# A two-layer network on one core: last output products begun early, expert weights loaded early, scatters spaced, sixteen wide products ahead of the attention

## The chip, the core and the metric

The kernel runs on one core of one Trainium2 chip. The metric is the device time of one execution in microseconds; three runs of the kernel before gave 2939.88, 2945.26 and 2947.61 us, median 2945.26 us. TensorE (PE) multiplies matrices, VectorE (DVE) and ScalarE (ACT) work element by element, GpSimd (POOL) does some products and the indirect transfers, SyncE (SP) issues the other transfers. Each engine runs its own list of instructions in order; they meet at semaphores.

## What is computed

Two layers on an input of 4 batches x 1024 tokens x 256 values. Everything is in float32.

```python
h = layernorm(x) * (1 + ca) + sa
x = x + ga * mamba(h)            # layer 0: state-space scan, 512 inner channels, 16 states
h = layernorm(x) * (1 + cb) + sb
x = x + gb * moe0(h)             # 8 experts, hidden 384, top 2
h = layernorm(x) * (1 + ca) + sa
x = x + ga * attention(h)        # layer 1: 8 heads of 128, causal, T = 1024
h = layernorm(x) * (1 + cb) + sb
x = x + gb * moe1(h)             # 16 experts, hidden 512, top 2, 640 slots each
```

The last step of the state-space layer is `y @ W_out`. In the second expert layer each token's normalised row goes, with its weights and its number, to two slots of a table in device memory; expert e reads its 640 slots, and adds its results to the tokens' rows of the output.

## The kernel before

Five phases follow one another, with a meeting of all engines between them: the state-space layer (`phase_mamba`, up to 973 us), routing of layer 0 (`phase_route`), its experts (`phase_experts0`, up to 1377 us), the attention with the routing of layer 1 inside it (`phase_attention`, 1377 to 2624 us), and the experts of layer 1 (`phase_experts1`, to the end). In each phase the order of every engine's work is written out by hand.

**State-space layer.** The 4096 tokens are 8 chunks of 512 columns (`CHUNKS`), two for each batch. A chunk has 64 scan steps (`STEPS`); step s takes the accumulator bank `da_ps[s % 4]`. VectorE scans and multiplies by C into `hc`, TensorE sums the results into `y_ps` (`sum_states`), ScalarE copies them out (`take_y`), TensorE turns them (`turn_back`), ScalarE copies again (`take_back`), GpSimd multiplies by the gate (`gate_y`, L796, one call for each half of the 512 inner channels), and `out_product` (L472) multiplies by W_out: for each of 4 token tiles, 4 products of 256 columns and one with the identity that adds x, in the banks `proj_ps`. `take_out` (L664) copies a pair of tiles back to x. For a chunk that isn't the last all this lies beside the next chunk's scan; for the last one it stands at the end of the phase, and `store_x` and the meeting of the engines follow.

**Attention, start.** SP issues four loads of 512 KB, for each half of batch 0 one from `sums0` (to `sh.x`) and one from `more0`, which are to be added; their semaphores are `x_first[0]` and `x_first[1]`. Behind them come the modulation rows (1.5 MB), `gate_w` (16 KB), `pos` (512 KB), `w_o` (1 MB, L1745) and batch 1's rows (1 MB). VectorE's `stats(0, j)` adds tile j and takes its statistics, for 8 tiles; then variance, root, reciprocal; then `normalise_rows` makes the 8 tiles' rows (a ring of 4). TensorE's list in this phase begins with these waits, ahead of everything else it does:

```python
pe.wait_ge(sh.att_w_in, 16)     # L1827
pe.wait_ge(S["w_o_in"], 16)     # L1828
```

Then it waits for `gate_w`, turns the 8 tiles' rows (`turn_rows`, L1837, two products of 128 columns a tile in one bank, which ScalarE copies to `h_b` before the next), and starts `project` (L1906) with eight products of 512 columns for the first head's q and k. The profile shows each float32 product as two instructions (these eight are "x16"), and each turn (transpose) as one.

**Attention, a batch.** Four batches, batches 1 and 2 being two turns of one loop. A batch has N = 64 steps n (8 heads x 8 row tiles): TensorE `score(n)`, VectorE `maximum(n)` (L2276), ScalarE the exponential, VectorE the division, TensorE `turn(n)`, ScalarE the copy (L2064), TensorE `weigh` (L1946). Between them stand the next batch's rows (`turn_rows`, from n = 56) and the routing of the batch before. The latter ends in `slots` at n = 54; then GpSimd's `scatter(b - 1)` (L1798) issues 16 indirect transfers of 128 rows each (L1803) in one go and waits until they have landed. After the last step `output` multiplies by `w_o`. Batch 3's own rows are routed in a tail, with 16 more scatters, and then the phase ends.

**Second expert phase, start.** SP issues the gate rows (512 KB, into `sh.mods[:, 2]`), then for experts 0 and 1 the slots (`xs`, 650 KB) and the two weights (512 KB each). TensorE turns the 5 slot tiles of expert 0 (L1546) and then multiplies (`hidden`, L1557).

## Time and profile before

The profiled execution took 2948.64 us, its span (first to last instruction) is 2946.9 us; this is 3.4 us above the median of the three runs.

| what | value |
|---|---|
| runs of the kernel before | 2939.88 / 2945.26 / 2947.61 us |
| profiled execution | 2948.64 us, span 2946.9 us |
| mean granted TensorE clock | 0.931 of full |
| busy: PE, DVE, ACT, POOL | 85%, 71%, 44%, 42% |
| phases end at | 973, 1377, 2624, 2947 us |

Busy time is summed over the span. Idle time of an engine matters only where another one waits for it, so the argument goes by stretches in order of time. A granted clock of 1.00 is 2.4 GHz, one of 0.50 is 1.2 GHz. In the rows, "[5.35 <-issue]" is the engine's idle time before the instruction and what ended it; "remote" is a semaphore event for which the profile has no instruction at that time.

### The profile page before, as it was taken

To read this page: it belongs to the slowest core of one execution; us is meant where nothing else is said; L and a number is where in the kernel's file an instruction comes from. 1 tells how busy PE (TensorE), PEld (TensorE's weight loads), DVE (VectorE), ACT (ScalarE), POOL (GpSimd) and SP (SyncE) were. 2 spreads that over 40 slices of the span, in tenths; PEclk is the share of its full clock that TensorE was granted. 3 is DMA by queue.
4 is the path that set the end of the run, shared out by engine and by line. 5 is a ranking of instruction groups with operands and counts; after the bars stand their busy time and mean duration, and the time that the engine had idled before them with its cause. 6 is when DMAs were issued, how large, how long until landed. Compare 5 with 4: busy or idle time off the path is not lost.

```text
span 2946.9 us, 39189 instructions
## 1 busy us (share of the span) xinstructions
PE 2494.0 (85%) x12341; PEld 1785.8 (61%) x12342; DVE 2104.0 (71%) x4277; ACT 1296.8 (44%) x2563; POOL 1234.6 (42%) x531
## 2 busy tenths in 40 slices
PE   6667777877866679996999999989998999859998
PEld 4355555555555469995566666556665666547776
DVE  4999999999999566665667477737774667455554
ACT  4667777677765245553343234313432343211111
POOL 2799999999997046664000000100001000223444
PEclk8889989888977889998999999999999999869999
DMA  4645655654655434345000100000000000035554
GB/s 146 202 151 177 194 169 171 196 167 168 201 171 165 161 104 63 63 63 140 18 1 1 45 3 1 18 28 19 1 6 28 15 1 1 29 108 128 129 129 73
DMA packets 150845, 268.98 MB, mean 91 GB/s; under 512 B 18316, under 2 KB 107324, under 8 KB 150172
## 3 DMA queue, kind: packets, MB, share of 16 engines
q1 hardware_dynamic: 121916, 227.12, 24.2%
q0 software_dynamic: 28224, 37.78, 7.7%
q8 instruction: 81, 1.33, 0.2%
q10 hardware_dynamic: 544, 2.10, 0.2%
q14 instruction: 80, 0.66, 0.1%
HBM read 209.52 MB, written 57.43 MB: 91 GB/s over the span
## 4 chain that ended last, share of the span: by engine, by line
PE 44%; DVE 3%; issue 2%; another core or an unknown queue 1%; ACT 1%; DMA 1%; POOL 0%; DVEq 0%; SPq 0%; ACTq 0%; POOLq 0%
PE at_o_ps L1946 8%; PE at_s_ps L1922 8%; PE at_qk_ps L1906 6%; PE e_h_ps L1557 5%; PE e_y_ps L1568 5%; PE at_s_ps L1954 4%; PE at_pt_ps L1933 4%; PE at_qk_ps L1911 3%; PE at_s_ps L1906 1%; DVE at_small L2276 1%; PE e_x_ps L1546 0%; PE at_s_ps L1911 0%; PE at_qk_ps L1837 0%; PE at_qk_ps L1852 0%
## 5 line engine op out<-in xcount | busy, mean ns | idle before, releaser
L765 POOL TENSOR_TENSOR dbx<-u,b_all 128x2048 f32<-128x2048 f32 x128 | 578.6, 4535 | 69.6 <-DVE u L844 34.1
L1803 POOL DMA_INDIRECT slots<-at_r_rows,slot_of x64 | 63.0, 984 | 1179.3 <-DVE slot_of L2218 1084.1
L2064 ACT COPY at_pt<-at_pt_ps 128x512 f32<-128x512 f32 (+3 forms) x384 | 172.2, 483 | 543.0 <-PE at_pt_ps L1933 507.6
L649 ACT ACTIVATE da_ps<-delta,a_neg 128x512 f32<-128x512 f32 x512 | 347.9, 689 | 134.9 <-DVE hc L917 126.7
L469 PE MATMUL y_ps<-ident,hc 128*128 128x128 f32 x1536 | 241.6, 301 | 90.7 <-DVE hc L917 90.2
L1922 PE MATMUL at_s_ps<-at_qk 128*128 128x512 f32 (+3 forms) x768 | 293.9, 492 | 3.3 <-DVE at_v L2267 3.1
L1946 PE MATMUL at_o_ps<-at_pt,at_v 128*128 128x512 f32 (+3 forms) x768 | 294.0, 495 | 0.0
L469 PEld LDWEIGHTS y_ps<-ident,hc 128*128 128x128 f32 x1536 | 196.0, 155 | 144.9 <-DVE hc L917 117.5
L2053 ACT ACTIVATE at_probs<-at_s_ps,at_small 128x128 f32<-128x128 f32 (+7 forms) x256 | 192.1, 751 | 202.0 <-DVE at_small L2278 201.6
L917 DVE TENSOR_TENSOR hc<-da_ps,c_all 128x512 f32<-128x512 f32 x384 | 257.0, 671 | 0.0
L907 DVE TENSOR_TENSOR_SCAN da_ps<-da_ps,state,dbx 128x512 f32<-128x512 f32 x192 | 243.0, 1275 | 6.1 <-ACT da_ps L649 4.3
L907 DVE TENSOR_TENSOR_SCAN da_ps<-da_ps,dbx 128x512 f32<-128x512 f32 x192 | 231.8, 1216 | 11.4 <-ACT da_ps L649 7.8
L2274 DVE TENSOR_TENSOR at_s_ps<-at_s_ps,at_later 128x128 f32<-128x128 f32 x256 | 75.9, 297 | 210.2 <-PE at_s_ps L1922 193.7
L1922 PEld LDWEIGHTS at_s_ps<-at_qk 128*128 128x128 f32 x768 | 138.1, 192 | 129.2 <-issue 97.1
L1906 PE MATMUL at_qk_ps<-at_h_b,w_qkv 128*128 128x512 f32 x448 | 211.9, 595 | 1.5 <-DVE at_rank L2204 0.9
L1534 POOL DMA_INDIRECT out<-e_ys,e_row_i x80 | 125.3, 1566 | 193.6 <-DVE e_ys L1643 164.4
L2276 DVE TENSOR_REDUCE at_small<-at_s_ps 128x1 f32<-128x128 f32 (+7 forms) x256 | 194.0, 758 | 8.8
L1933 PE MATMUL at_pt_ps<-ident,at_probs 128*128 128x128 f32 x1152 | 171.2, 276 | 32.8 <-ACT at_pt L2064 11.7
L1933 PEld LDWEIGHTS at_pt_ps<-ident,at_probs 128*128 128x128 f32 x1152 | 137.6, 142 | 98.9 <-issue 78.5
L1946 PEld LDWEIGHTS at_o_ps<-at_pt,at_v 128*128 128x128 f32 x768 | 129.3, 194 | 61.2 <-issue 58.3
L1591 ACT ACTIVATE e_hid<-e_h_ps 128x320 f32<-128x320 f32 x128 | 56.0, 437 | 249.5 <-PE e_h_ps L1557 249.0
L1568 PE MATMUL e_y_ps<-e_w,e_hid 128*128 128x256 f32 x640 | 152.3, 382 | 5.6 <-ACT e_hid L1591 5.6
(385 smaller groups left out, 5003.8 us busy)
## 6 DMA issues: line engine op xcount, KB each, us to landing
b_all<-bc_rows SPq DMA_DIRECT2D x128, 512.0 KB, 4.5
c_all<-bc_rows SPq DMA_DIRECT2D x128, 512.0 KB, 5.1
e_w<-L_ffn_w SPq DMA_DIRECT2D x32, 512.0 KB, 5.5
slots<-zeros SPq DMA_DIRECT2D x40, 260.0 KB, 6.3
e_xs<-slots SPq DMA_DIRECT2D x16, 650.0 KB, 7.1
w<-L_ffn_W SPq DMA_DIRECT2D x24, 384.0 KB, 8.4
more<-zeros SPq DMA_DIRECT2D x16, 256.0 KB, 5.0
sums<-x SPq DMA_DIRECT2D x8, 512.0 KB, 6.9
```

The lines of the kernel that those rows point to most:

```text
L469: mm = nc.tensor.matmul(y_ps[par][:, at], source[:, at], sh.ident[:], start=False, stop=(last and j == CT - 1), is_transpose=True)
L649: nc.scalar.activation(da_ps[s % RING_DA][:], delta[:, c % 2, m, :], ACT.Exp, scale=sh.a_neg[:, m, n:n + 1]).then_inc(S["da_ready"], 1)
L765: nc.gpsimd.tensor_tensor(dbx[:, at % RING_DBX], pair, rows, ALU.mult).then_inc(S["dbx_ready"], 1)
L907: nc.vector.tensor_tensor_scan(out, h, dbx[:, at % RING_DBX, i // 2, par, :], 0.0 if c % CPB == 0 else state[:, s:s + 1], ALU.mult, ALU.ad ...
L917: nc.vector.tensor_tensor(hc[:, v % RING_H, :], da_ps[s % RING_DA][:], c_all[:, at % RING_C, s % GS // 2, :], ALU.mult).then_inc(S["hc_rea ...
L1568: last = nc.tensor.matmul(y_ps[(r + t) % 2][:], hid[:, m, t * P:(t + 1) * P], w2[:, r, m, :], start=(m == 0), stop=(m == MF1 - 1))
L1906: last = nc.tensor.matmul(out, w_qkv[:, k, h, i // 2, :], h_b[:, i % 2, k, :], start=(k == 0), stop=(k == KE - 1))
L1922: last = nc.tensor.matmul(s_ps[n % 2][:, part * CH:end], qk[:, h % 2, 0, i * P:(i + 1) * P], qk[:, h % 2, 1, part * CH:end], start=True, s ...
L1933: last = nc.tensor.transpose(pt_ps[half][:, j % CT, :], probs[:, n % 3, j * P:(j + 1) * P], sh.ident[:])
L1946: last = nc.tensor.matmul(o_ps[:, first:], v[:, h % 2, j, :], pt[half][:, j, first:], start=(j == 0), stop=(j == (half + 1) * CT - 1))
L2053: nc.scalar.activation(probs[:, n % 3, 0:(i + 1) * P], s_ps[n % 2][:, 0:(i + 1) * P], ACT.Exp, bias=small[:, n % 4, 1:2], scale=SCALE, acc ...
L2276: nc.vector.reduce_max(small[:, n % 4, 0:1], s_ps[n % 2][:, 0:(i + 1) * P], AX_X).then_inc(S["max_taken"], 1)
```

## The change

1. State-space layer, last chunk: of each token tile's five products the three that don't need the second half of the gated values (x by the identity, two of the four W_out products) are issued earlier, into `da_ps[0]` and `da_ps[1]`: tiles 0 and 1 after the summing of steps 61 and 62, tiles 2 and 3 after `turn_back`. After the last gating only two products for each tile are left. `take_out` of that chunk reads `da_ps`.
2. Attention, start: SP waits for `x_first[1]` before it issues the modulation rows and what follows. VectorE adds the first half in one operation of 1024 columns, GpSimd the second half. TensorE gets 16 products of 512 columns (`WARM`) on `w_qkv`, whose results nobody reads, between its first waits (L1827, L1828) and its wait for `gate_w`.
3. Attention, batches 1 to 3: before scattering tile j of the batch before, GpSimd waits until `score` of step 54 + j is done (`SLOTS[2]` is 54).
4. The weights of experts 0 and 1 and the gate rows of the second expert phase go to the room of `w_qkv`, and are loaded in batch 3, when the last `project` is done; SP waits for them before the phase ends. In the second expert phase SP then issues only the slots for experts 0 and 1.

The diff, without lines that only rename:

```diff
@@ phase_mamba, tensor
+            def last_first_blocks(j):
+                pair, i = j // 2, j % 2
+                if i == 0:
+                    pe.wait_ge(S["hc_ready"], hc_at(LAST, STEPS - RING_DA + pair) + 1)
+                    pe.wait_ge(S["y_gated"], LAST * HALVES + 1)
+                    pe.wait_ge(S["w_ready"], B)
+                out = da_ps[pair][:, i * E:(i + 1) * E]
+                nc.tensor.matmul(out, sh.ident[:], sh.x[:, LAST * CT + j, :], start=(i == 0), stop=False, skip_group_check=True)
+                for k in range(2):
+                    nc.tensor.matmul(out, u[:, LAST % 2, k, j * P:(j + 1) * P], sh.w_out[:, k, :], start=False, stop=False, skip_group_check=True)
+
+            def last_blocks(pair):
+                if pair == 0:
+                    pe.wait_ge(S["y_gated"], CHUNKS * HALVES)
+                for i in range(2):
+                    j = pair * 2 + i
+                    for k in range(2, MD):
+                        mm = nc.tensor.matmul(da_ps[pair][:, i * E:(i + 1) * E], u[:, LAST % 2, k, j * P:(j + 1) * P], sh.w_out[:, k, :],
+                                              start=False, stop=(k == MD - 1), skip_group_check=True)
+                mm.then_inc(S["out_done"], 1)
...
                     sum_states(c, k)
+                    if c == LAST and k >= STEPS - 3 and k < STEPS - 1:
+                        last_first_blocks(k - STEPS + 3)
...
-                turn_back(CHUNKS - 1, m)
+                turn_back(LAST, m)
+            for j in range(2, CT):
+                last_first_blocks(j)
             for pair in range(2):
-                out_product(CHUNKS - 1, pair)
+                last_blocks(pair)
@@ phase_experts1, sync
-            sp.dma_start(sh.mods[:, 2], d["mod_rows"][1, 5].partition_broadcast(P)).then_inc(mods_in, 16)
...
-                if not early(e, 2):
-                    sp.wait_ge(y_done, (e - 1) * S1)
+                if early(e, 2):
+                    return
+                sp.wait_ge(y_done, (e - 1) * S1)
@@ phase_attention, sync
+            sp.wait_ge(x_first[1], 32)
             load_mods(sp, d, sh, 1, 0, S["mods_in"])
...
             store_out(B - 2)
+            sp.wait_ge(S["qk_done"], B * HEADS * PIECES + 1)
+            sp.dma_start(sh.gates[:], d["mod_rows"][1, 5].partition_broadcast(P)).then_inc(sh.gates_in, 16)
+            for e in range(2):
+                sp.dma_start(sh.w1[:, e], d["L1_ffn_w1"][e].rearrange("(k p) f -> p k f", p=P)).then_inc(sh.w1_in[e], 16)
+                sp.dma_start(sh.w2[:, e], d["L1_ffn_w2"][e].rearrange("(m p) f -> p m f", p=P)).then_inc(sh.w2_in[e], 16)
             store_out(B - 1)
@@ phase_attention, gpsimd
+            late = slice(CT, TPB)
+            pool.wait_ge(x_first[1], 32)
+            nc.gpsimd.tensor_tensor(sh.x[:, late], sh.x[:, late], more[:, late], ALU.add).then_inc(first_summed[1], 1)
...
                 for j in tiles:
                     i = rb * TPB + j
+                    if count is None:
+                        pool.wait_ge(S["scored"], (rb + 1) * N + SLOTS[2] + 1 + j)
@@ phase_attention, tensor
             pe.sem_inc(S["rows_left"], 1)
+            for i in range(WARM):
+                nc.tensor.matmul(s_ps[0][:, 0:CH], w_qkv[:, 0, 0, 0, :], w_qkv[:, 0, 0:2, 0:2, :], start=True, stop=True)
             pe.wait_ge(S["gate_in"], 16)
@@ phase_attention, vector
+            early = slice(0, CT)
+            dve.wait_ge(x_first[0], 32)
+            nc.vector.tensor_tensor(sh.x[:, early], sh.x[:, early], more[:, early], ALU.add).then_inc(first_summed[0], 1)
             for j in range(TPB):
-                stats(0, j)
+                if j % CT == 0:
+                    dve.wait_ge(first_summed[j // CT], 1)
+                nc.vector.bn_stats(sh.stats[:, j, :], sh.x[:, j, :]).then_inc(S["stats_in"], 1)
+            dve.sem_inc(S["summed"], TPB)
```

## Rows read from the trace of the kernel before

**Rows 1.** The page's chain that ended last, shares of the span.

```profile
PE 44%; DVE 3%; issue 2%; another core or an unknown queue 1%; ACT 1%; DMA 1%; POOL 0%; DVEq 0%; SPq 0%; ACTq 0%; POOLq 0%
```

**Rows 2.** Order of time, first phase's end: start us, us, engine, line.

```profile
958.61 2.34 POOL L796 TENSOR_TENSOR u<-u,gate 128x1024 f32<-128x1024 f32 x1 [13.08 <-ACT u L581]
...
961.00 3.49 PE L479 MATMUL proj_ps<-w_out,u 128*128 128x256 f32 x8 [3.09 <-POOL u L796]
...
971.44 0.58 ACT L667 COPY x<-proj_ps 128x512 f32<-128x512 f32 x1 [3.73 <-PE proj_ps L481]
```

**Rows 3.** Stretch, length, busy us (instructions) by engine, granted clock, DMA.

```profile
961.00:964.20 3.20, 3.20 (x8) 2.62 (x9) 0.00 (x0) 0.00 (x0) 0.00 (x0) 0.52 0.00 0
964.20:971.30 7.10, 7.10 (x34) 6.00 (x32) 0.75 (x2) 0.58 (x1) 0.00 (x0) 1.00 0.00 0
```

**Rows 4.** TensorE in order of time, short bursts.

```profile
919.04 0.66 PE L469 MATMUL y_ps<-ident,hc 128*128 128x128 f32 x4 [1.12 <-DVE hc L917]
921.47 1.12 PE L469 MATMUL y_ps<-ident,hc 128*128 128x128 f32 x4 [1.77 <-DVE hc L917]
```

**Rows 5.** Transfers at the attention's start: KB, us to landing.

```profile
x<-sums SPq DMA_DIRECT2D x1, 512.0 KB, 3.9
...
at_attn<-more SPq DMA_DIRECT2D x1, 512.0 KB, 7.4
...
at_w_o<-woT SPq DMA_DIRECT2D x1, 1024.0 KB, 12.9
```

**Rows 6.** The attention's start in order of time.

```profile
1379.01 0.51 SPq L1741 DMA_DIRECT2D at_attn<-more  x1
...
1381.67 0.44 SPq L1745 DMA_DIRECT2D at_w_o<-woT  x1
...
1392.38 0.48 DVE L2243 SCALAR_TENSOR_TENSOR at_rows<-at_rows,rstd,mods 128x256 f32<-128x256 f32 x1
...
1394.96 0.66 PE L1837 MATMUL at_qk_ps<-ident,at_rows 128*128 128x128 f32 x2 [24.46 <-DVE at_rows L2243]
...
1404.57 8.72 PE L1906 MATMUL at_s_ps<-at_h_b,w_qkv 128*128 128x512 f32 x16 [0.46 <-ACT at_h_b L2039]
```

**Rows 7.** Batch 1, in order of time, while batch 0 is scattered.

```profile
1901.80 1.05 POOL L1803 DMA_INDIRECT slots<-at_r_rows,slot_of  x1 [521.99 <-DVE slot_of L2218]
...
1911.30 0.38 PE L1837 MATMUL at_qk_ps<-ident,at_rows 128*128 128x128 f32 x2
...
1912.78 1.09 PE L1933 MATMUL at_pt_ps<-ident,at_probs 128*128 128x128 f32 x8 [0.24 <-issue]
...
1919.71 0.58 ACT L2064 COPY at_pt<-at_pt_ps 128x512 f32<-128x512 f32 x1 [6.05 <-remote]
...
1921.44 0.96 POOL L1803 DMA_INDIRECT slots<-at_r_rows,slot_of  x1 [0.30 <-issue]
...
1924.73 0.69 DVE L2290 COPY at_attn<-at_o_ps 128x512 f32<-128x512 f32 x1 [6.59 <-remote]
```

**Rows 8.** Row maximum of steps 54 and 63, batches 0, 1, 3.

```profile
1612.29 1.09 DVE L2276 TENSOR_REDUCE at_small<-at_s_ps 128x1 f32<-128x896 f32 x1
...
1641.36 1.23 DVE L2276 TENSOR_REDUCE at_small<-at_s_ps 128x1 f32<-128x1024 f32 x1
...
1902.82 1.09 DVE L2276 TENSOR_REDUCE at_small<-at_s_ps 128x1 f32<-128x896 f32 x1
...
1944.14 1.23 DVE L2276 TENSOR_REDUCE at_small<-at_s_ps 128x1 f32<-128x1024 f32 x1
...
2505.30 1.09 DVE L2276 TENSOR_REDUCE at_small<-at_s_ps 128x1 f32<-128x896 f32 x1
...
2546.58 1.23 DVE L2276 TENSOR_REDUCE at_small<-at_s_ps 128x1 f32<-128x1024 f32 x1
```

**Rows 9.** The second expert phase's start in order of time.

```profile
2624.31 0.43 SPq L1507 DMA_DIRECT2D e_xs<-slots  x1
...
2630.45 1.12 PE L1546 MATMUL e_x_ps<-ident,e_xs 128*128 128x128 f32 x4 [23.57 <-DMA e_xs<-slots]
```

More of the change, by code:

```diff
@@ L482, in out_product @@
                 mm.then_inc(S["out_done"], 1)
+            LAST = CHUNKS - 1
+            def last_first_blocks(j):
[17 more added lines that the diff above has]
+                mm.then_inc(S["out_done"], 1)
             pe.wait_ge(S["c_ready"], 1)
@@ L666, in take_out @@
                 act.wait_ge(S["out_done"], c * 2 + pair + 1)
-                nc.scalar.copy(sh.x[:, tile:tile + 2, :], proj_ps[pair][:].rearrange("p (i e) -> p i e", i=2)).then_inc(S["out_added"], 1)
+                bank = da_ps[pair] if c == CHUNKS - 1 else proj_ps[pair]
+                nc.scalar.copy(sh.x[:, tile:tile + 2, :], bank[:].rearrange("p (i e) -> p i e", i=2)).then_inc(S["out_added"], 1)
             act.dma_start(wmod[0], d["L0_wmod"].rearrange("(k p) f -> p k f", p=P)).then_inc(wmod_in[0], 16)
@@ L1464, in phase_experts1 @@
         sem = sh.kept("e1_")
-        w1 = sb("w1", [P, 2, KE, F1])
-        w2 = sb("w2", [P, 2, MF1, E])
+        w1, w2, gates = sh.w1, sh.w2, sh.gates
         xs = sb("xs", [P, 2, S1, ROW])
@@ L1478, in phase_experts1 @@
         y_ps = [ps(f"y_ps{i}", [P, E]) for i in range(2)]
-        w1_in, w2_in, x_in = ([sem(f"{n}{i}") for i in range(2)] for n in ("w1_in", "w2_in", "x_in"))
-        mods_in, consts_ready, steps_set, meta_chain, gate_chain, rows_set, added = (
-            sem(n) for n in "mods_in consts_ready steps_set meta_chain gate_chain rows_set added".split())
+        w1_in, w2_in, x_in = sh.w1_in, sh.w2_in, [sem(f"x_in{i}") for i in range(2)]
+        consts_ready, steps_set, meta_chain, gate_chain, rows_set, added = (
+            sem(n) for n in "consts_ready steps_set meta_chain gate_chain rows_set added".split())
         x_turned, x_copied, h_done, h_act, y_done, y_copied = (sem(n) for n in "x_turned x_copied h_done h_act y_done y_copied".split())
@@ L1622, in gate_rows @@
             def gate_rows(e, r, b):
-                before = sh.mods[:, 2, 0, :]
+                before = gates[:, 0, :]
                 for t in range(S1):
@@ L1646, in body @@
                     read_meta(e + 1, 1 - r, q + r)
-            dve.wait_ge(mods_in, 16)
+            dve.wait_ge(sh.gates_in, 16)
             for b in range(1, B):
-                nc.vector.tensor_tensor(sh.mods[:, 1, b, :], sh.mods[:, 2, b, :], sh.mods[:, 2, b - 1, :], ALU.subtract).then_inc(steps_set, 1)
+                nc.vector.tensor_tensor(sh.mods[:, 1, b, :], gates[:, b, :], gates[:, b - 1, :], ALU.subtract).then_inc(steps_set, 1)
             dve.wait_ge(consts_ready, 2)
@@ L1708, in phase_attention @@
         x_first = [sem(f"x_first{th}") for th in range(CPB)]
+        first_summed = [sem(f"first_summed{th}") for th in range(CPB)]
         names = ("x_in summed route_in gate_in stats2_in stats2_chain var2_ready std2_ready rstd2_ready r_half_ready r_row_ready r_turned_done "
@@ L1716, in phase_attention @@
         block = ctx.enter_context(nc.Block(no_gpsimd_drain=True))
+        WARM = 16
         ADD = tuple(4 + 2 * j for j in range(TPB))
@@ L1769, in _ @@
             store_out(B - 2)
+            sp.wait_ge(S["qk_done"], B * HEADS * PIECES + 1)
[3 more added lines that the diff above has]
+                sp.dma_start(sh.w2[:, e], d["L1_ffn_w2"][e].rearrange("(m p) f -> p m f", p=P)).then_inc(sh.w2_in[e], 16)
             store_out(B - 1)
             sp.wait_ge(S["x_stored"], 16 * B)
+            sp.wait_ge(sh.gates_in, 16)
+            for e in range(2):
+                sp.wait_ge(sh.w1_in[e], 16)
+                sp.wait_ge(sh.w2_in[e], 16)
         @block.gpsimd
@@ L2114, in stats @@
                 tile = nb * TPB + j
-                if isinstance(nb, int) and nb == 0:
-                    dve.wait_ge(x_first[j // CT], 32)
-                else:
-                    dve.wait_ge(S["x_in"], nb * 32)
+                dve.wait_ge(S["x_in"], nb * 32)
                 nc.vector.tensor_tensor(sh.x[:, tile, :], sh.x[:, tile, :], more[:, j, :], ALU.add).then_inc(S["summed"], 1)
@@ L2478, in program @@
             phase_experts0(nc, d, sh)
+        place = sh.w_qkv[:].rearrange("p k h c f -> p (k h c f)")
+        sh.w1 = place[:, 0:2 * KE * F1].rearrange("p (r k f) -> p r k f", r=2, k=KE)
+        sh.w2 = place[:, 2 * KE * F1:2 * KE * F1 + 2 * MF1 * E].rearrange("p (r m e) -> p r m e", r=2, m=MF1)
+        sh.gates = place[:, 2 * KE * F1 + 2 * MF1 * E:2 * KE * F1 + 2 * MF1 * E + B * E].rearrange("p (b e) -> p b e", b=B)
+        sh.w1_in, sh.w2_in = ([sh.kept("e1_")(f"{n}{i}") for i in range(2)] for n in ("w1_in", "w2_in"))
+        sh.gates_in = sh.kept("e1_")("gates_in")
         phase_attention(nc, d, sh)
```

## The prediction

> **What bounds the kernel now.** I read the chain that ended last first: no engine but TensorE holds a large share of it [rows 1]. So an edit pays where TensorE waits, and by no more than that wait. Then I read four places in order of time, those that the change touches: the end of the first phase [rows 2, 3], the start of the attention [rows 5, 6], the end of each batch, where the rows of the batch before are scattered [rows 7, 8], and the start of the last phase [rows 9]. The reader is to see in each what released TensorE, and at which of its two clocks it then worked: [rows 3] has 8 instructions of 256 columns in 3.20 us at a granted clock of 0.52 (0.4 each), and 34 in 7.10 us at 1.00 (0.21 each). A float32 product is two such instructions.
>
> **Part 1, last output products.** Before, TensorE starts them at 961.00, released by the gating on GpSimd, and ScalarE starts the last copy at 971.44: 10.4 us for 40 instructions [rows 2]. After it, 8 products (16 instructions) are left: 3.4 us at full clock plus 0.2 to the copy. The other 12 products of W_out and x move ahead. Those of tiles 0 and 1 stand between the sums of steps 61, 62 and 63: 6 instructions of 0.215 = 1.3 us twice, of which TensorE's waits there take up some; the last sum, the copy, the turn and the gating come later by about 1.7 us. Those of tiles 2 and 3 (2.6 us) lie beside the gating of 2.34 us [rows 2] and keep TensorE at work, so that the clock, which fell there before, stays. Sum: 1.7 + 3.4 + 0.2 - 10.4 = -5 us. Bounds: -1.7 if the clock falls all the same (16 x 0.4 = 6.9), -6 if the early products delay the gating by less. The next phase starts earlier by as much, nothing else waits.
>
> **Part 2, the attention's start.** Who released TensorE's first turns at 1394.96? The profile names VectorE's row, but that row started at 1392.38 and took 0.48, so it had been ready for 2 us [rows 6]. The transfer of `w_o`, issued at 1381.67, took 12.9 us: it landed at 1394.6 [rows 5, 6]. TensorE's list begins with the wait for it (L1828). That wait stays, and the 16 products stand behind it, not in the time in which TensorE is idle. So they are on the path.
> When does `w_o` land now? The loads of batch 0 end at 1379.01 + 7.4 = 1386.4; before, what followed was queued already, now it is issued only then. The first load of 512 KB took 3.9 us from issue [rows 5]; it was issued 1.5 us ahead of the fourth, so it landed at 1381.4, and the other three followed at 1.7 us each. So about 2.2 us of the 3.9 are start-up. `w_o` lands at 1396.9, TensorE starts at 1397.2. The new adding doesn't reach so far: GpSimd's operation of 128x1024 takes 2.34 us [rows 2], so it is done at 1388.8; before, adding, statistics, variance and the first row together took from the landing at 1386.4 to 1392.9 [rows 5, 6], and 6.5 us from 1388.8 is 1395.3, still ahead of `w_o`.
> The 16 products are 32 instructions of 512 columns. By [rows 3], doubled, one takes 0.85 us at half clock and 0.43 at full. A model of the start stands in [rows 6]: the first 16 of `project` take 8.72 us from an idle engine, which is 4 of 0.85 and 12 of 0.43 and the end of the last one. So 3.4 + 28 x 0.43 = 15.4 us, to 1412.7. What do they give back? A turn of two instructions takes 0.66 us cold [rows 6] and 0.38 warm [rows 7]; with ScalarE's copy a tile takes 1.21 and would take 0.93, so 8 tiles save 2.2 us if the clock holds, and the first 16 instructions of `project` would take 6.9 instead of 8.6. But the clock doesn't hold in such sparse work: in [rows 4] four turns of 128 columns stand alone with idle time of 1.1 and 1.8 us ahead of them, at 919.04 at full clock (0.66) and at 921.47 at half (1.12). I take half of the first gain and none of the second: 8 x 1.07 = 8.6, then 8.6: 1429.9, where before it was 1404.57 + 8.56 = 1413.1. That is +16.8; with all gained back it is +13.9, with `w_o` no later +11.6, with nothing gained back +17.8. I take +16. Behind it TensorE is the bound, so it is not given back.
>
> **Part 3, the scatters.** From [rows 8]: from the row maximum of step 54 to that of step 63 batch 0 takes 29.1 us, batch 1 41.3, batch 3 41.3 (batch 2 repeats it). Batch 0 alone has no scatters. The excess is 12.2 us three times, 37 us. [Rows 7] show it: 16 transfers are issued back to back, 1.3 us apart, from 1901.80 to 1922.4. Nothing is late in the first 9 us. Then TensorE's turns of 1912.78 end at 1913.9, and ScalarE, idle for 6 us, copies them at 1919.71; VectorE is idle for 6.6 us until 1924.73, which is 2.3 us after the last issue has ended. In the view of waits, those that end "remote" occur nowhere in the kernel but in these three stretches. I read it as TensorE's signals being delayed by an unbroken run of scatters.
> By the change the first four go at once (5 us), then GpSimd waits for step 56 (about 4 us), then each pair of 2.5 us is let go by a step; batch 0's steps are 29.1 / 9 = 3.2 us apart, those of the short row tiles (56 to 59) less, I estimate 2.5. So there is another nearly unbroken run of about 8, and if signals are late then, `score` is late too, GpSimd stops within one pair and the delay clears in the 2.3 us seen above. I put what is left at one such episode, 3 us a batch. Sum: 3 x (3 - 12.2) = -28 us. Bounds: -37 with nothing left; 0 if spacing doesn't matter. The rows are scattered later (the last pair at step 61), but the next user of `r_rows` comes 30 steps on. A gain below this one isn't possible: nothing else of it is on TensorE's path.
>
> **Part 4, early weights.** SP waits for the last `project` of batch 3 with only the store of that batch behind it, which is due after `output`; 2.5 MB lie under the attention, and at worst make batch 3's scatters slower. In the last phase the slots are issued first, 0.4 us sooner, and alone: before, the issue at 2624.31 released TensorE at 2630.45, after 6.1 us [rows 9]; the first load of 512 KB in [rows 5] took 3.9, so 650 KB take some 4.3. -2 us, between -0.4 and -2.3; the weights were never late.
>
> **Sum.** -5 + 16 - 28 - 2 = -19 us on 2948.6 gives 2929.6 for such an execution; the profiled one lies 3.4 us above the median, so 2926 us.
>
> **The rivals**, all on the median.
> The stall goes wholly: part 3 gives -37, total -28, 2917 us. For it: the first eight transfers in a row delayed nothing [rows 7]. Against: some eight come in a row again.
> The stall is tied to a place in the order of instructions (code that has to be fetched, say), and scatters only lengthen it: then the run at steps 56 to 58 meets it as before and only the end of the run is cut, about -15, total -6, 2939 us. For it: it begins at about the same steps in all three batches.
> Spacing changes nothing and the 16 products cost what they cost: part 3 gives 0, total +9, 2954 us, slower than before. It decides from the point where part 3 gives less than 9 us, which is what the other parts cost together. For it: between two pairs GpSimd hardly pauses from step 56 to 59. Against: the pauses before it, and that `score` holds the scatters back.
> A worse form: every one of the six later pairs delays one signal by 2.4 us or more, so that the steps and the scatters hold each other up; 17 us a batch instead of 12.2, total +23, 2968 us.
> The Trainium skill (SBUF — State Buffer, section Who interferes with whom) says that a DMA never contends with a compute engine, and that PE and ACT wait on nobody. By it the scatters couldn't stall TensorE or ScalarE, spacing them would give 0 and the kernel would come to the 2954 us of the third rival; the rows speak against the rule as far as signals are concerned, since the same steps take 12 us more only beside scatters.
>
> **How the numbers follow.** Chances: forecast 0.42, stall gone 0.28, tied to a place 0.12, nothing from spacing 0.11, worse form 0.07. A measurement of this kernel tells 0.3% (8.8 us) from no change. Faster by more: the first two, and a little of the third, 0.73. Within: the rest of the third and half of the fourth, 0.14. Slower: 0.13. The range is to hold the first three: its low end is -37 with +12, -6 and -2, so 2911; its high end is the third with +18 at the start, 2942. With a margin for both, 2909 to 2943 us.
>
> **What the profile would show.** Part 1: TensorE starts on `da_ps` at about 962.7 and the last copy at 966.3, clock 1.00. Part 2: 32 instructions of 512 columns starting at 1397, not before 1394; `project` ends its 16 at about 1430 less what part 1 gave (5). If they start at 1378, the wait was not what I took it for, and part 2 is near -1. Part 3: the steps 54 to 63 of batches 1 to 3 in 32 us, "remote" waits gone or one of 2 to 4 us each, scatters in pairs. 41 us there would make the forecast wrong by itself. Part 4: the last phase's first turn 4 to 5 us after its first issue.

## The result, and the profile after

The changed kernel took 2920.78 us (median of 4 runs, 2920.41 to 2922.07), the kernel before 2944.66 us in the same comparison (4 runs, 2939.88 to 2947.61): ratio 0.992, 95% interval 0.9907 to 0.9934. That is 23.9 us less; forecast were 19 less, 2926.0 us. The profiled executions span 2920.4 and 2946.9 us, so 26.5 us have to be found in the two traces.

A later experiment showed that this result doesn't hold on every chip: on another the same changed kernel is 10.9 us slower than the kernel before. Both are told below, the first comparison first.

Where the 26.5 us went, from the first transfer of each stage to that of the next:

| stage | before | after | difference |
|---|---|---|---|
| first phase, up to its last copy (ScalarE) | 971.44 | 970.82 | -0.6 |
| from there to the attention's first transfer | 406.1 | 404.2 | -1.9 |
| from there to the product group behind the first `project` | 35.6 | 55.1 | +19.4 |
| from there to the last phase's first transfer | 1210.8 | 1169.6 | -41.2 |
| from there to the first hidden product | 10.2 | 8.0 | -2.2 |

**First phase's end.** The changed kernel in order of time (start us, us, engine, line); these rows answer to [rows 2].

```profile
957.79 1.27 DVE L935 TENSOR_TENSOR_SCAN da_ps<-da_ps,state,dbx 128x512 f32<-128x512 f32 x1
...
964.65 2.35 POOL L824 TENSOR_TENSOR u<-u,gate 128x1024 f32<-128x1024 f32 x1 [14.68 <-ACT u L608]
...
967.06 3.72 PE L503 MATMUL da_ps<-w_out,u 128*128 128x256 f32 x16 [0.51 <-POOL u L824]
...
970.82 0.59 ACT L695 COPY x<-da_ps 128x512 f32<-128x512 f32 x1 [1.14 <-PE da_ps L503]
```

16 instructions are left behind the gating instead of 40, and they run in 3.72 us, so at full clock. From the scan of step 63 to the last copy it is 13.0 us; before, the same scan stood at 953.36, 18.1 us ahead of the copy at 971.44. That is the gain of 5 us. But the scan itself stands 4.4 us later than before, in code that the change doesn't touch (2.8 us of it are there at 253 us, all of it at 595 us); so only 0.6 us is left in this pair of executions. Such a difference says nothing of the change: over the 14 profiled executions of this document that scan starts anywhere between 953.3 and 957.8 us. From it to the last copy it is 18.1 to 19.4 us in the nine that have the old end of this phase, and 13.0 to 13.3 in the five that have the new one.

**The attention's start**, in order of time; these rows answer to [rows 6].

```profile
1374.98 0.37 SPq L1768 DMA_DIRECT2D x<-sums  x1
...
1385.55 0.48 SPq L1774 DMA_DIRECT2D at_w_o<-woT  x1
...
1391.29 0.48 DVE L2286 SCALAR_TENSOR_TENSOR at_rows<-at_rows,rstd,mods 128x256 f32<-128x256 f32 x1
```

TensorE alone:

```profile
1395.98 16.86 PE L1936 MATMUL at_s_ps<-w_qkv 128*128 128x512 f32 x32 [27.71 <-DMA at_w_o<-woT]
1412.67 0.38 PE L1881 MATMUL at_qk_ps<-ident,at_rows 128*128 128x128 f32 x2
1413.61 0.41 PE L1881 MATMUL at_qk_ps<-ident,at_rows 128*128 128x128 f32 x2 [0.55 <-ACT at_h_b L2085]
...
1419.38 0.66 PE L1881 MATMUL at_qk_ps<-ident,at_rows 128*128 128x128 f32 x2 [0.55 <-ACT at_h_b L2085]
1420.51 9.69 PE L1952 MATMUL at_s_ps<-at_h_b,w_qkv 128*128 128x512 f32 x16 [0.46 <-ACT at_h_b L2085]
```

The wide products stand behind the transfer of `w_o`, as the profile now says itself, and the first normed row, finished at 1391.8, waits for them until 1412.67. What the clock did (stretch, length, busy us (instructions) of each engine, granted clock, DMA):

```profile
1395.90:1401.90 6.00, 5.92 (x7) 2.53 (x8) 0.00 (x0) 0.00 (x0) 0.00 (x0) 0.51 0.88 281
1401.90:1412.60 10.70, 10.70 (x26) 4.70 (x25) 0.00 (x0) 0.00 (x0) 0.00 (x0) 1.00 0.00 0
1412.60:1419.40 6.80, 2.93 (x16) 1.39 (x14) 3.75 (x8) 2.61 (x7) 0.00 (x0) 0.96 0.10 32
...
1421.00:1425.00 4.00, 4.00 (x6) 1.42 (x6) 0.57 (x1) 0.76 (x1) 0.00 (x0) 0.50 0.52 183
```

The products do raise the clock to its upper level (1.00 of 2.4 GHz) and the turns have it nearly to their end. But the turns keep TensorE busy for 2.93 us of 6.80 only, the clock falls at their end, and `project` starts at the lower level: its 16 instructions take 9.69 us, against 8.72 in [rows 6].

**The scatters.** The row maxima of steps 54 and 63 of batches 1 and 3 on VectorE, in order of time; these rows answer to [rows 8].

```profile
1919.74 1.09 DVE L2325 TENSOR_REDUCE at_small<-at_s_ps 128x1 f32<-128x896 f32 x1
...
1948.03 1.23 DVE L2325 TENSOR_REDUCE at_small<-at_s_ps 128x1 f32<-128x1024 f32 x1
...
2495.74 1.09 DVE L2325 TENSOR_REDUCE at_small<-at_s_ps 128x1 f32<-128x896 f32 x1
...
2522.02 1.23 DVE L2325 TENSOR_REDUCE at_small<-at_s_ps 128x1 f32<-128x1024 f32 x1
```

28.3, 28.3 and 26.3 us in batches 1 to 3 instead of 41.3, 41.8 and 41.3: 41.2 us in all. No wait that ends "remote" is left in these stretches; a few signals of TensorE are still late there, the two worst by 1.1 and 1.3 us, in batch 3. Batch 3 is shorter than batch 0 (29.1), which has no scatters; so batch 0 was not the right measure of what an undisturbed batch takes.

**The last phase**, in order of time; these rows answer to [rows 9].

```profile
2599.66 7.89 SPq L1532 DMA_DIRECT2D e_xs<-slots  x3
...
2603.99 1.11 PE L1572 MATMUL e_x_ps<-ident,e_xs 128*128 128x128 f32 x4 [21.73 <-DMA e_xs<-slots]
```

4.3 us from issue to the first turn, against 6.1 before. The forecast had 4.3.

### The profile page after: what moved, and what is told of

Same layout as the page of the kernel before. It is cut to its first block and busy times, and to the rows that moved or that the text cites. A ratio compares the mean times of both kernels' runs of the same rounds, so it can differ in the third digit from the quotient of the medians.

```text
span 2920.4 us, 39254 instructions
## 1 busy us (share of the span) xinstructions
PE 2500.7 (86%) x12373; PEld 1788.7 (61%) x12374; DVE 2101.7 (72%) x4270; ACT 1297.2 (44%) x2563; POOL 1238.3 (42%) x532
## 5 line engine op out<-in xcount | busy, mean ns | idle before, releaser
L469 PE MATMUL y_ps<-ident,hc 128*128 128x128 f32 x1536 | 239.4, 300 | 83.6 <-DVE hc L945 82.8
L1979 PEld LDWEIGHTS at_pt_ps<-ident,at_probs 128*128 128x128 f32 x1152 | 136.1, 141 | 75.4 <-issue 52.2
L1979 PE MATMUL at_pt_ps<-ident,at_probs 128*128 128x128 f32 x1152 | 168.8, 274 | 11.7 <-DVE at_probs L2335 11.4
L802 POOL TENSOR_TENSOR own_h<-own_h,c_all 128x2048 f32<-128x2048 f32 x32 | 144.9, 4527 | 31.3 <-DVE own_h L935 31.3
```

The lines of the kernel that those rows point to most:

```text
L469: mm = nc.tensor.matmul(y_ps[par][:, at], source[:, at], sh.ident[:], start=False, stop=(last and j == CT - 1), is_transpose=True)
L1979: last = nc.tensor.transpose(pt_ps[half][:, j % CT, :], probs[:, n % 3, j * P:(j + 1) * P], sh.ident[:])
```

## The experiments

The kernels ran in four groups, each group on one chip of its own, with the kernel before timed beside it. The chip of the first comparison is called A, those of the groups B, C, D and E (whether A is one of the others isn't known). By "the hold" I mean what [rows 7] show: signals between engines that arrive some microseconds late beside a run of scatters, as waits that end "remote".

The traces also tell whose signals are late. Each semaphore event can be set beside the end of the last instruction that raises that semaphore. In the kernel before on A, from the first scatter of a batch to 4 us behind the last, 39 events of TensorE are recorded and 28 of them come over 0.3 us late, the worst 11.3 us; of the 78 of VectorE and ScalarE none does. In the eight traces from C, D and E none of TensorE's 635 is late. So it is TensorE's signals that are held, and no other engine's. (TensorE's ends are modelled by the profile, so how much of each delay lies ahead of the signal can't be told from them alone; run 2 speaks to that.)

### Chip B: which part brings what

**1. The spaced scatters alone**, added to the kernel before:

```
             for j in tiles:
                 i = rb * TPB + j
+                if count is None:
+                    pool.wait_ge(S["scored"], (rb + 1) * N + SLOTS[2] + 1 + j)
                 for k in range(2):
                     nc.gpsimd.indirect_dma_start(...)
```

> The kernel before with the spaced scatters alone: one added wait per token tile, nothing else of the change. My theory, that a long unbroken run of scatters delays the signals of the other engines: the row maxima of steps 54 and 63 lie about 28.3 us apart in all four batches (before 29.1, 41.3, 41.8, 41.3), the time falls by 41 us to about 2904 us. Rival, that the delay hangs on a place in the order of instructions and that other parts of the change (the shifted code, the products ahead of the attention) removed it: steps 54 to 63 still take 35 us or more in three batches, the time stays over 2925 us.

Measured 2908.11 us, the kernel before 2948.87 beside it: ratio 0.9865 (0.9849 to 0.9882), -40.8 us. Steps 54 to 63 take 29.4, 28.4 and 26.4 us. So this one wait brings what the whole change brought in these steps, and no other part of the change has a share in it. A remnant of the hold is still to be seen in batch 1, of 1.6 us, behind no more than four scatters in a row:

```profile
1917.15 0.27 ACT L2066 COPY at_pt<-at_pt_ps 128x128 f32<-128x128 f32 x1 [1.59 <-remote]
1917.29 0.96 POOL L1805 DMA_INDIRECT slots<-at_r_rows,slot_of  x1 [1.08 <-remote]
```

**2. One unbroken run, begun later.**

```
+                if count is None and j == 0:
+                    pool.wait_ge(S["scored"], (rb + 1) * N + 63)
```

> The kernel before, with all 16 scatters of a batch still in one unbroken run, but begun only once score 62 of the next batch is made (one wait ahead of the first scatter). My theory, unbroken run: steps 54 to 63 take 28.3 us, and the delay comes back behind step 63, in the output products and the first products of the batch behind; the time stays within 12 us of the kernel before. Rival, place in the order of instructions (steps 54 to 63 are what is delayed, by whatever runs beside them): nothing is delayed later, the time falls by some 41 us to about 2904 us. Second rival, sheer number of scatters beside the steps: also no gain from spacing alone, which the first run answers.

Measured 2911.4 us, ratio 0.9881 (0.9865 to 0.9898): -37.5 us, where my theory wanted the delay back behind step 63. By its time alone the rival had won. The trace (end of the run of scatters in batch 1, order of time) says otherwise:

```profile
1928.66 1.01 POOL L1805 DMA_INDIRECT slots<-at_r_rows,slot_of  x1 [549.14 <-PE at_s_ps L1924]
...
1938.13 7.17 PE L1956 MATMUL at_s_ps<-at_w_o,at_attn 128*128 128x256 f32 x32 [1.60 <-issue]
...
1945.15 5.75 PE L1948 MATMUL at_o_ps<-at_pt,at_v 128*128 128x512 f32 x16
...
1948.25 0.96 POOL L1805 DMA_INDIRECT slots<-at_r_rows,slot_of  x1 [0.30 <-issue]
1951.65 0.42 DVE L2418 TENSOR_TENSOR at_gated<-at_s_ps,mods 128x256 f32<-128x256 f32 x1 [6.83 <-remote]
```

VectorE waits for the second group of output products, which TensorE ended at 1945.3 before it went straight on to other work; so here TensorE isn't held, its signal is. VectorE is held for 6.8 us until 2.4 us behind the end of the last issue, as at 1924.73 in [rows 7], where it was 2.3. The same is seen in batch 2 (6.8 us) and in batch 3 (4.4 us), and nothing is held in steps 54 to 63 (28.7, 28.7 and 25.4 us). So the hold went with the scatters, away from the steps: it isn't tied to a place in the order of instructions. It cost only 0.8 us there (from the maximum of step 63 to the first of the next batch 53.0 instead of 52.2), since TensorE worked on through it: the output products go into four banks in turn, and VectorE catches up. In steps 54 to 63 TensorE, VectorE and ScalarE hand every tile to each other, and TensorE itself comes to stand, as in batch 1 of the kernel before (TensorE alone):

```profile
1914.27 0.81 PE L1922 MATMUL at_s_ps<-at_qk 128*128 128x384 f32 x2
1920.44 0.45 PE L1933 MATMUL at_pt_ps<-ident,at_probs 128*128 128x128 f32 x1 [5.35 <-issue]
```

The expectation was right in the mechanism and wrong in the price.

**3. Without the wide products** (`WARM = 0` in the changed kernel).

> The changed kernel without the sixteen wide products. My theory: they run whole behind the wait for w_o and on the path, so the turned rows begin as soon as w_o lands (21 us behind the attention's first transfer), are turned at half clock in 1.21 us each as before, and the projections that follow take 8.7 us: the next product group begins about 16 us earlier, time about 2905 us. Rival: the products were hidden, since rows, mods or w_o would have held the turned rows as long, or a higher clock behind them repays them: time within 4 us of the changed kernel, 2917 to 2925 us.

Measured 2904.66 us, ratio 0.9856 (0.9839 to 0.9872). The changed kernel wasn't in this group, so the price is read in the trace, from the attention's first transfer:

| us from the first transfer to | first turn | `project` | next product group |
|---|---|---|---|
| kernel before (A) | 17.5 | 27.1 | 35.6 |
| changed kernel (A) | 37.7 | 45.5 | 55.1 |
| changed kernel (D) | 36.0 | 44.2 | 52.9 |
| without wide products (B) | 20.9 | 30.5 | 39.3 |
| and wait for `w_o` late (B) | 16.5 | 26.1 | 35.5 |
| wide products, wait for `w_o` late (C) | 17.9 | 26.0 | 35.2 |

Without the products the start is 15.8 us shorter than in the changed kernel on A and 13.6 shorter than on D: they were wholly on the path. TensorE's row without them:

```profile
1391.45 0.66 PE L1881 MATMUL at_qk_ps<-ident,at_rows 128*128 128x128 f32 x2 [27.78 <-DMA at_w_o<-woT]
...
1401.06 8.98 PE L1952 MATMUL at_s_ps<-at_h_b,w_qkv 128*128 128x512 f32 x16 [0.46 <-ACT at_h_b L2085]
```

**4. Without them, and the wait for `w_o` where `w_o` is read.**

```
-            pe.wait_ge(S["w_o_in"], 16)
...
                     if t == 0:
+                        if first_batch:
+                            pe.wait_ge(S["w_o_in"], 16)
                         pe.wait_ge(S["exp_done"], b * N + N - 1)
```

> The changed kernel without the sixteen wide products, and with TensorE's wait for w_o moved from the attention's start to its first output product, where w_o is first read. My theory: the start is then held by the first normed row, ready 16.8 us behind the attention's first transfer instead of 21.0 for w_o: about 4 us below the changed kernel without wide products, 20 us below the changed kernel, about 2901 us. Rival: another transfer (the gate's weights, the modulation rows) holds TensorE as long as w_o did: time as without the wide products, about 2905 us.

Measured 2901.03 us, ratio 0.984 (0.9823 to 0.9856), 3.6 us below run 3. TensorE's first turn is now really released by the row, which the profile had named in the kernel before too:

```profile
1389.90 0.66 PE L1880 MATMUL at_qk_ps<-ident,at_rows 128*128 128x128 f32 x2 [23.24 <-DVE at_rows L2287]
```

So the wait for `w_o` had cost 4.4 us of the start (20.9 against 16.5). In the kernel before it was 2.1: the first row ready at 15.4, the turn at 17.5 [rows 6]; the changed order of loads had doubled it.

### Chip C: wide products that do lie beside the loads, and a surprise

**5. Run 4 with its wide products.**

> The changed kernel with its sixteen wide products kept, and TensorE's wait for w_o moved from ahead of them to the first output product, so that they start at once and really lie beside the loads. My theory: 16.9 us of products from the phase's start end about when the first normed row is ready (16.5 us behind the first transfer); the turns behind them run at full clock, 0.96 us each instead of 1.21, for some 7 us, which gives at most 2 us back, and the clock falls before the projections as in the changed kernel: the same time as without wide products, 2901 us within 2 us. Rival: the full clock holds into the projections, and the start is 4 us or more shorter: below 2898 us. Second rival: they end later than the first row and cost 3 us or more: above 2904 us.

Measured 2898.73 us (7 runs, 2896.44 to 2902.62). TensorE in order of time:

```profile
1374.51 16.50 PE L1935 MATMUL at_s_ps<-w_qkv 128*128 128x512 f32 x32 [8.50 <-issue]
1390.85 0.38 PE L1880 MATMUL at_qk_ps<-ident,at_rows 128*128 128x128 f32 x2
...
1398.88 9.41 PE L1951 MATMUL at_s_ps<-at_h_b,w_qkv 128*128 128x512 f32 x16 [0.46 <-ACT at_h_b L2086]
```

The turns take 8.0 us instead of 9.6, but start 1.4 us later, and `project` is as slow as without (9.3 us to the next product group, 9.4 in run 4): 0.3 us gained in all (35.2 against 35.5). The first theory holds in the trace; the time lies 0.3 us below the stretch that it gave (2901 us within 2), and most of the distance to run 4 is the chip, for the rest of the attention takes 3.2 us less here than in run 4, which had a remnant of the hold. Even where they lie beside the loads, the wide products bring next to nothing, because the clock falls in the sparse turns before the dense work begins.

The surprise was the kernel before: 2907.2 us on this chip (10 runs, 2904.85 to 2909.28), 37 to 42 us less than on A and B. Run 5 gains 8.5 us on it, ratio 0.9973 (0.9961 to 0.9984).

**6 to 8. Three patterns to find what the hold depends on:** twelve scatters and four, a filler behind each scatter (`nc.gpsimd.memset(filler[:], 0.0)`), and 64 rows in each scatter (`sh.slot_of[0:64, k, i:i + 1]`, `r_rows[0:64, j, :]`; half of the rows aren't stored).

> The kernel before, with twelve scatters of a batch unbroken (15 us) and the last four held until score 60 of the next batch. My theory (signals of other engines are held from about 10 us into an unbroken run to about 2.4 us behind its last scatter): the hold begins as before but ends some 5 us earlier, so steps 54 to 63 take 33 to 35 us in batches 1 to 3, between the 28.3 of the spaced kernel and the 41.3 of the kernel before; about 2925 us. Rival, a place in the order of instructions or an effect of the total number: 28 to 29.5 us or 40 us or more.

> The kernel before, with no wait for scores, but one short fill of a scratch tile of 128x256 behind each scatter on the same engine (0.3 us), so that the scatters start every 1.6 us instead of 1.27 and never stand directly behind each other. Theory A, the average rate counts (about what the spaced kernels have, 16 in 26 us): no signal is held, steps 54 to 63 take 28 to 29.5 us, about 2908 us. Theory B, only real pauses of the engine count (a wait of 0.65 us or more each pair): signals are still held, steps 54 to 63 take 38 us or more, over 2935 us.

> The kernel before, with each scatter of batches 0 to 2 writing 64 rows instead of 128, so that half of those rows are never stored; still 16 scatters back to back. If the number of rows (descriptors, written one by one) fills something up: a scatter takes less time and the hold vanishes, steps 54 to 63 take 28 to 30 us, about 2908 us. If each scatter instruction counts whatever its rows: its duration stays near 0.96 us with a pitch of 1.27 us, and steps 54 to 63 stay at 41 us, about 2948 us.

Measured 2909.62, 2909.19 and 2907.71 us, one run each. Steps 54 to 63: 28.6, 28.8 and 25.4 us; 29.1, 29.2 and 25.6; 28.9, 28.8 and 25.4. As the kernel before ran without the hold too, none of the three tells anything of its cause. The last has all sixteen scatters unbroken, 1.2 us apart, with nothing late; so not the pattern made the difference to A and B, but the chip (or something else that changed from group to group with it).

### Chip D: the changed kernel where the hold is missing

**9. The changed kernel once more, and 10. twelve and four once more.**

> The changed kernel itself, once more. In the call before this one the kernel before took 2907 us on its chip instead of 2945 to 2949, so the hold of signals during the scatters seems to be missing on some chips. Theory: what the change does to the attention's start, the last output products and the last phase (worked out from the traces: +19.4, -6.9 and -2.2 us) is there on every chip, and only the 41 us of the scatters depends on the chip. If this chip has the hold (kernel before 2940 us or more), the changed kernel takes 2919 to 2923 us, 24 to 28 us less than the kernel before; if it has not (kernel before near 2907 us), the changed kernel takes 2917 to 2921 us and is 10 to 14 us slower than the kernel before. Rival: the difference between the chips lies elsewhere and both kernels move alike: the changed kernel near 2883 us where the kernel before takes 2907.

> Twelve scatters unbroken, the last four held until score 60, once more, since the chip of its first run showed no held signals at all. If this chip has the hold: steps 54 to 63 take 33 to 35 us in batches 1 to 3 if signals are held from about 10 us into an unbroken run to about 2.4 us behind its last scatter (about 2925 us); 28 to 29.5 us if the hold is tied to a place or to the number of sixteen. If this chip has no hold: 28.7 us and 25.4 us in the last batch, as in the first run, about 2909 us.

The kernel before took 2908.23 us (10 runs), so this chip lacks the hold as well. The changed kernel took 2919.1 us (7 runs, 2914.89 to 2920.71): ratio 1.0035, interval 1.0024 to 1.0047. It is slower, by 10.9 us, as the first theory had it. Its rows, TensorE at the attention's start and VectorE's maxima of steps 54 and 63 of batch 1:

```profile
1391.08 15.61 PE L1936 MATMUL at_s_ps<-w_qkv 128*128 128x512 f32 x32 [27.44 <-DMA at_w_o<-woT]
1406.53 0.38 PE L1881 MATMUL at_qk_ps<-ident,at_rows 128*128 128x128 f32 x2
...
1414.75 8.87 PE L1952 MATMUL at_s_ps<-at_h_b,w_qkv 128*128 128x512 f32 x16 [0.46 <-ACT at_h_b L2085]
```

```profile
1913.15 1.09 DVE L2325 TENSOR_REDUCE at_small<-at_s_ps 128x1 f32<-128x896 f32 x1
...
1941.80 1.23 DVE L2325 TENSOR_REDUCE at_small<-at_s_ps 128x1 f32<-128x1024 f32 x1
```

The steps take 28.7 us, in batch 3 25.4, with spacing as without it. Twelve and four took 2905.34 us (one run), steps 28.6, 28.6 and 25.4: again nothing on the cause. But its trace is that of the kernel before on this same chip in all but the scatters, so the two can be set side by side: their spans are 2903.6 and 2913.2 us, the changed kernel 9.6 longer. Up to the attention's first transfer it gains 6.4, its start costs 17.0 more (52.9 against 35.9), the rest of the attention gains 0.2, the last phase's start 1.7, and what follows takes 0.9 more. The profiled execution is the fastest of the seven, 4.2 us below their median, so this doesn't settle the 10.9 to the last microseconds.

### Chip E: one pattern for each batch

**11 and 12.** To get six patterns out of two kernels, each batch had its own.

> The kernel before with another pattern of scatters in each batch. Batch 1: twelve unbroken, four held until score 60. Batch 2: no wait, one fill of a 128x256 scratch tile (0.33 us) behind each scatter, a start every 1.6 us. Batch 3: eight unbroken (10 us), eight held until score 60. On a chip that shows the hold (kernel before 2940 us or more, steps 54 to 63 in 41 to 42 us in the kernel before): if signals are held from about 10 us into an unbroken run to 2.4 us behind its last scatter, steps 54 to 63 take 33 to 35 us in batch 1, and 26 to 28 us in batch 3; in batch 2 28.7 to 30 us if a lower rate is enough, 38 us or more if only real pauses of the engine are. If the hold is tied to steps 54 to 63 whatever runs beside them, 38 us or more in all three. On a chip without it (kernel before near 2907 us): 28.7, 29.2 and 25.4 us.

> The kernel before with its own pattern in batch 1 (all sixteen unbroken), 64 rows instead of 128 in each scatter of batch 2 (the other half of the rows of that batch isn't stored), and in batch 3 all sixteen unbroken but begun at score 57 instead of about score 54. On a chip that shows the hold: batch 1 takes 41 to 42 us for steps 54 to 63; batch 2 takes 28 to 31 us if the number of rows fills something up, 40 us or more if each scatter counts whatever its rows; batch 3 takes 28 to 36 us with the rest of the hold behind step 63 if the hold goes with the run of scatters, 25 to 27 us if it is tied to the steps and these have passed. On a chip without it: 28.7, 28.8 and 25.4 us.

The kernel before took 2908.04 us, the two 2907.19 and 2906.75. Steps 54 to 63: 28.6, 29.2 and 25.4 us in the first, 28.9, 28.8 and 25.4 in the second: no hold, in any pattern. (The second doesn't store half of the rows of one batch.) Batch 1 of the second has the pattern of the kernel before. Its first and last scatter, and a maximum between them (order of time):

```profile
1901.23 1.05 POOL L1806 DMA_INDIRECT slots<-at_r_rows,slot_of  x1 [522.15 <-DVE slot_of L2221]
...
1918.72 0.69 DVE L2279 TENSOR_REDUCE at_small<-at_s_ps 128x1 f32<-128x512 f32 x1
...
1920.94 1.03 POOL L1806 DMA_INDIRECT slots<-at_r_rows,slot_of  x1 [0.30 <-issue]
```

The scatters are as long and as close together as in [rows 7] (16 in 20.7 us, there in 20.6), and the maximum of step 59 comes at 1918.72, where on chip A the same instants passed in waits. So is what they move: in both traces 768 packets belong to these sixteen scatters, of 124 ns on average, and the last ends 1.1 us behind the last issue. What differs is only when TensorE's signals arrive.

## Why the prediction was right, and where it was not

The forecast lay 5.2 us above the measured time, within its range, and the sign was right. It stands on two terms that were both too small in size, and of opposite sign, so that it came this close is partly luck. The larger luck is the chip: on D the same forecast would have had the wrong sign.

**Part 1, last output products: right.** Forecast -5, measured -5.0 from the scan of step 63 to the last copy. It is hidden in the first comparison by 4.4 us that the unchanged code before it lost. Two slips in its working change nothing: 16 x 0.4 is 6.4 and not 6.9, and by their own terms the ends of the range are 2912 and 2941, ahead of the margin. (What [rows 4] show, read as turns under part 2, are the sums of the scan's states.)

**Part 2, the attention's start: the mechanism right, the size off.** That `w_o` was the real releaser and that the products stand behind it was right, and run 4 shows it. Forecast +16, measured +19.4, above the upper bound of 17.8. Term by term: `w_o` released TensorE 21.0 us behind the first transfer, forecast 19.7 (+1.3); the 32 instructions took 16.7 us, forecast 15.4 (+1.3), since the lower clock lasted for 7 instructions and not 4; the turns took 7.8 us, forecast 8.6 (-0.8); `project` took 9.5 us, forecast 8.6 (+0.9). The bound "nothing gained back" missed that `project` could become slower than before. With 16.8 for the sum these make 19.5 (I had taken 16). On chip D the last three are 15.5, 8.2 and 8.7 us, 32.4 in all where the forecast had 32.6, and `w_o` came at 20.6. So some 2 us of the miss lie in where the clock changed in that execution, and 1 us in `w_o`.

**Part 3, the scatters: the reason right for this chip, the size too small.** Forecast -28, measured -41.2 and, alone, -40.8. The step that failed is "some eight come in a row again, 3 us a batch are left". In batches 1 and 2 no more than four come in a row: GpSimd pauses 0.6 to 2.4 us between the later pairs on A. In batch 3 eight do come in a row, and even there only some 0.9 us are left (26.3 us against 25.4 on D); on B a batch keeps at most 1.4 us (30.1 in batch 2 of run 4 against 28.7). The reading behind it, that nothing is late in the first 9 us of a run of scatters, holds for batch 1 alone: the first late signals of TensorE come 11.4, 7.2 and 5.7 us into the runs of batches 1 to 3. The second error stood in the measure: batch 0 takes 29.1 us for these steps, undisturbed batches 28.7 and 25.4 (D), so the excess in [rows 8] was some 12.6, 13 and 16 us, not 12.2 three times. The bound of -37 was therefore no bound. The rival "the stall goes wholly" was the right one, at 2917 us; in the traces, part 2 (3.4 us more) and the later first phase (4.4) on the one side, part 3 (4 us more) and the phases between (1.9) on the other, leave the result 1.5 us above it, and the profiled execution of the changed kernel lies only 1.3 us above its median where that of the kernel before lay 3.4.

**Part 4, early weights: right.** Forecast -2, measured -2.2.

**What no row of one trace could show.** I forecast the stall as something the kernel does. It is something that the kernel does on some chips: it was there on A and B (perhaps one chip) and missing on C, D and E. On the last three the rival "spacing changes nothing" holds (in effect, if not for its reason): it gave +9 us for the rest of the change, and 10.9 were measured on D. The evidence for "tied to a place" is gone: run 2 moved the hold. One form of it, code that has to be fetched, has more against it. The profile has transfers of instructions of 16 KB, one about every 26 us in this phase. The one that comes at 1917.2 in run 1 comes at 1927.2 in the kernel before, behind the run of scatters, which looks like a cause; but in run 2 they come at 1916.5 and 1939.2, the second in the middle of the run of scatters and no later than in run 1 (1939.3), and the hold is there all the same.

The Trainium skill (SBUF — State Buffer, section Who interferes with whom) says that a DMA never contends with a compute engine and that PE and ACT wait on nobody. On C, D and E the traces agree: 28.9 us with unbroken scatters, 28.7 with spaced ones. On A and B they don't, if signals are counted in: ScalarE and VectorE stood for 6 to 9 us beside scatters. But the section is about the ports of the memory, and what came late here were TensorE's signals: the scatters' packets took the same 124 ns on A as on E.

**What stays open** is the cause of the hold: why it shows on some chips, what in a run of scatters brings it on (length, rate, rows), and whether it belongs to the chip at all. Each chip was met in one group of runs only, so the core, the place of the tables in memory or the hour may have changed with it. All the patterns made to tell the rest apart (runs 6 to 8 and 10 to 12) met chips without the hold. The length of an unbroken run alone isn't it: four in a row are followed by late signals on B (run 1, batch 1), and eight in a row cost under 1 us on A (changed kernel, batch 3). That TensorE's signals in particular are late, which I read from [rows 7], is borne out by the counts above.

**The version to keep** is run 5 or run 4: the last output products, the spaced scatters and the early weights of the change, and the wait for `w_o` at its use. It takes 2901.03 us where the kernel before takes 2948.87 (B), and 2898.73 where that takes 2907.2 (C): each is faster than the kernel before where it ran, one on a chip with the hold and one on a chip without, and both lie below the changed kernel's 2920.78 (A) and 2919.1 (D). The spacing alone brings the kernel before on B to 2908.11, just what it takes elsewhere without it; it is an insurance whose price is within 1 us by the steps (28.7, 28.7 and 25.4 us with it on D, 28.9 unspaced in batch 1 on E).

## What to carry to other kernels

A wait in an engine's list comes due where it stands, not where its data is read: before anything is put "into the idle time", look at which wait ends it and on which side of that wait the new work stands. Raising TensorE's clock ahead of sparse work was lost here before the dense work started; whether it pays directly ahead of dense work, no run here tested. And a stall whose waits end in nothing that the kernel owns should be seen on a second chip before it is priced: here one stage was worth 41 us on one or two chips and nothing on three others, and the sign of the whole change hung on it.

## What was not expected of the hardware

The kernel before takes 2944.66 and 2948.87 us on A and B, and 2907.2, 2908.23 and 2908.04 us on C, D and E, with scatters of the same length. For steps 54 to 63 of batches 1 to 3 it takes 124.4 us on A; kernels that differ from it only in their scatters take 82.8 (run 6) and 83.1 (run 8) on C. The last held wait ends 2.3 to 2.9 us behind the end of the last scatter's issue in each of the six batches that show it (A and run 2), whether that comes at 1922.4 or at 1949.2, and in the output products it costs 0.8 us where VectorE shows 6.8 us of waiting.

Behind the wide products TensorE's clock stayed at its upper level (2.4 GHz) for 6.3 us of single turns on A (granted 0.96 over 6.80 us) and then fell to the lower (1.2 GHz); on D it fell after some 4.9 us of them (the first turn takes 0.38 us, the sixth 0.54, the seventh 0.66). Only TensorE's signals come late under the hold; VectorE's, ScalarE's and the scatters' own packets don't.
